# Dealing GpSimd's power and multiplication of the q and k norms out over three turns of an attention pipeline

## The reference

```python
q = (x @ Wq).reshape(b, n, H, DH).transpose(0, 2, 1, 3)
k = (x @ Wk).reshape(b, n, H, DH).transpose(0, 2, 1, 3)
...
q = l2norm(q)
k = l2norm(k)
dots = jnp.einsum('bhid,bhjd->bhij', q, k) * QK_SCALE
dots = jnp.einsum('hg,bgij->bhij', W_pre_th, dots)
...
top = jax.lax.top_k(dots, TOPK)[0]
vk = top[..., -1:]
dots = jnp.where(dots < vk, mask_value, dots)
attn = jax.nn.softmax(dots, axis=-1)
attn = jnp.einsum('hg,bgij->bhij', W_post_th, attn)
```

## Time and profile before

| | us |
|---|---|
| median of 3 runs | 2283.63 (2280.85 to 2287.51) |
| the profiled execution | 2286.81 |
| its span, first to last instruction | 2285.0 |
| attention's first and last power (L1381) start | 220.7 and 1937.9 |

### The profile page before, as it was taken

One profiled execution on the slowest core, in us unless ns is written; L12 is line 12 of the kernel. 1 busy time (PEld: TensorE's weight loads), 2 busy tenths in 40 slices (PEclk: granted clock), 3 DMA queues, 4 the chain that ended last, 5 costly groups with the idle time before them and its releaser, 6 DMA issues. The chain is left out here.

```text
span 2285.0 us, 55636 instructions
## 1 busy us (share of the span) xinstructions
PE 2040.8 (89%) x16059; PEld 1325.7 (58%) x16060; DVE 1765.2 (77%) x6818; ACT 1602.4 (70%) x4676; POOL 938.0 (41%) x2739
## 2 busy tenths in 40 slices
PE   7995799899989998899899988998899889974997
PEld 3433456666666666666666666666666666663433
DVE  6565389968996899689968996899689958984346
ACT  4442589858985888589768875897689768951542
POOL 3001455454544554555355435553554356321000
PEclk9997799999999999999999999999999999997998
DMA  6002012111211121112111211121112101302002
GB/s 180 0 0 88 18 46 63 44 26 44 63 44 26 44 63 44 26 44 63 44 27 44 63 44 26 45 62 44 26 45 63 44 24 48 70 24 89 1 0 74
DMA packets 113219, 104.72 MB, mean 46 GB/s; under 512 B 34448, under 2 KB 110864, under 8 KB 112912
## 3 DMA queue, kind: packets, MB, share of 16 engines
q1 hardware_dynamic: 108000, 96.65, 16.6%
q10 hardware_dynamic: 4912, 4.46, 0.6%
HBM read 19.14 MB, written 12.71 MB: 14 GB/s over the span
## 5 line engine op out<-in xcount | busy, mean ns | idle before, releaser
L1054 PE MATMUL bankC<-R,E 128*128 128x128 f32 x2560 | 352.0, 287 | 46.9 <-POOL R L1416 46.9
L1054 PEld LDWEIGHTS bankC<-R,E 128*128 128x128 f32 x2560 | 338.3, 202 | 85.1 <-POOL R L1416 51.8
L1038 PE MATMUL bankB<-raw,mixpre 128*128 128x76 f32 (+37 forms) x1024 | 354.7, 434 | 20.4 <-DMA raw<-SC 20.3
L1254 ACT ACTIVATE S<-bankB,aim_first 128x68 f32<-128x68 f32 (+56 forms) x456 | 232.8, 514 | 87.8 <-PE bankB L1038 87.2
L1514 DVE TENSOR_SCALAR_CACHE_REDUCE S<-S,minus_thr 128x68 f32<-128x68 f32 (+56 forms) x456 | 217.7, 514 | 94.1 <-POOL minus_thr L1400 93.5
L1391 POOL TENSOR_TENSOR S<-S,diagmask 128x8 f32<-128x8 f32 x512 | 116.6, 233 | 409.1 <-ACT S L1254 353.0
L1568 DVE SCALAR_TENSOR_TENSOR E<-S,limit,E 128x68 f32<-128x68 f32 (+56 forms) x456 | 234.1, 549 | 37.6 <-ACT E L1280 9.0
L1416 POOL TENSOR_SCALAR R<-mixpost,rinv 128x128 f32<-128x128 f32 x512 | 187.6, 379 | 183.8 <-DVE rinv L1572 183.4
L1027 PE MATMUL bankD<-KT,QT 64*64 64x132 f32 (+8 forms) x2304 | 190.5, 405 | 66.5 <-ACT SC L1243 37.4
L1280 ACT ACTIVATE E<-S,nmax 128x12 f32<-128x12 f32 (+56 forms) x512 | 241.7, 535 | 0.0
L1080 PEld LDWEIGHTS bankM<-PT,V 128*64 128x64 f32 x5120 | 180.3, 138 | 97.9 <-issue 90.5
(11 more groups left out here) (178 smaller groups left out, 3927.7 us busy)
## 6 DMA issues: line engine op xcount, KB each, us to landing
X_first<-in_L_attn_x_dram ACTq DMA_DIRECT2D x8, 512.0 KB, 9.7
x<-X_first SPq DMA_DIRECT2D x8, 512.0 KB, 2.9
xt<-x SPq DMA_DIRECT2D x32, 128.0 KB, 2.3
x<-xt SPq DMA_DIRECT2D x32, 128.0 KB, 2.4
X_last<-x SPq DMA_DIRECT2D x8, 512.0 KB, 6.6
out_dram<-X_last SPq DMA_DIRECT2D x8, 512.0 KB, 2.8
raw<-SC SPq DMA_DIRECT2D x8, 258.0 KB, 3.0
raw<-SC SPq DMA_DIRECT2D x8, 254.0 KB, 3.0
```

Source lines behind the costliest of these rows:

```text
L1038: last = nc.tensor.matmul(bankB[n % 2][:, 0:wide(n)], W.mixpre[:, :], raw[n % RAWS][:, 0:wide(n)], start=True, stop=True)
L1054: last = nc.tensor.matmul(bankC[n % 2][:, jb * P:(jb + 1) * P], E[n % EBUFS][:, jb * P:(jb + 1) * P], R[n % RBUFS][:, :], start=True, stop ...
L1254: nc.scalar.activation(S[n % SBUFS][:, 0:wide(n)], src, ACT.Identity, bias=W.aim_first[:, group(n)]).then_inc(S_out, 1)
```

## The change

`norm` is cut in two: `inverse_norms` (wait for the sums, power) and `norm` (wait for the power and for the evicted projection, multiplication). In a tile the power of q stays in turn 2; the multiplication of q and the power of k stand in turn 4; the multiplication of k stands in turn 6. The work ahead of the loop keeps its order.

```diff
-            def norm(j, i):
+            def inverse_norms(j, i):
                 pool.wait_ge(ssq_done, 2 * j + i + 1)
                 nc.gpsimd.tensor_tensor(rn[:, i, :], ssq[:, i, :], W.neghalf[:, 0:H], ALU.pow).then_inc(rn_ready, 1)
+
+            def norm(j, i):
                 pool.wait_ge(rn_ready, 2 * j + i + 1)
                 wait_read(pool, ("qk"[i], j, 1))
                 v = qk[:, i, :].rearrange("p (h d) -> p h d", d=DH)
...
-            norm(0, 0)
-            norm(0, 1)
+            for i in range(2):
+                inverse_norms(0, i)
+                norm(0, i)
...
                     if g == 2:
                         copy_halo(t + 1)
+                        inverse_norms(t + 1, 0)
+                    if g == 4:
                         norm(t + 1, 0)
-                    if g == 4:
+                        inverse_norms(t + 1, 1)
+                    if g == 6:
                         norm(t + 1, 1)
```

## The result

| | before | changed |
|---|---|---|
| median of 4 runs, us | 2282.93 (2280.85 to 2287.51) | 2301.07 (2299.65 to 2304.03) |
| the profiled execution, us | 2286.81 | 2299.65 |
| its span, us | 2285.0 | 2297.9 |

The changed kernel takes 1.0078 of the time, with a 95% interval of 1.006 to 1.0097: it is **slower by some 18 us**. The forecast was 2315 us, slower by 31; the direction and the range (2292 to 2328) held, the step was forecast 1.7 times too large.

The account below looks back on a forecast made before the run. VectorE was taken to set the pace from late tile 1 through tile 3, TensorE in tile 0. Terms 9.6 + 6.8 + 11.3 + 3.6 = 31.3 us slower gave a median of 2315 us, range 2292 to 2328.

Parts of the forecast that it names:

- The mechanism: VectorE sets the pace from late tile 1 through tile 3; multiplications right behind R stall its non-scan instructions until they end.
- Rival (c): L1527 and L1532 not held at all, stalls of tiles 1 and 2 vanish: faster, 2269 us; chance 0.08.
- Rival (b): Only TensorE pays: stalls cancel, late transposition costs 0.45 and 0.85 us in tiles 0 and 1: 2294 us; chance 0.09.
- Rival (a): Trade one for one: as many multiplications stall VectorE as before, TensorE's gaps absorb the late transposition: about 2284 us; chance 0.13.
- Tile 1: Second tile of each batch element: q's stall nets nothing, k's multiplication costs 1.2 us, eight times: 9.6 us.
- Tile 2: Third tile: L1556 stall gone (-1.58), q's multiplication 1.3, k's at L1527 1.1; +0.85 us, eight times: 6.8 us.
- Tile 3: Widest tile: k's multiplication stalls L1527 0.86 us, q's costs 0.75 at L1490; 1.6 us, seven times: 11.3 us.
- The race at L1490: Tile 3: q's multiplication and L1490 start 0.04 us apart; stall of 1.69 us or nothing, 0.75 taken.
- In tiles 2 and 3 VectorE does not wait for them: Turn 4's nmax, masks and thresholds come 1.9 us earlier, but VectorE is not waiting there; no gain booked.
- tile 3 lengthened most: Sign of a right forecast in the new profile: tile 3 grows most, by 0.9 or 2.5 us.
- Tile 0: First tile, where TensorE sets the pace: its transposition waits 0.45 us for k's multiplication, eight times: 3.6 us.
- The power: GpSimd's 2.9 us power, run in turns 2 and 4, holds no VectorE instruction; priced at nothing on VectorE.

Follow-up runs that it names:

- q late alone: Changed kernel with the multiplication of k put back to turn 4 behind its power, only that of q later than before: 2310.37 us, ratio 1.012 to the kernel before.
- isolated run: Kernel before with the change made in one tile of four only: tiles 1 alone 2286.93 us (ratio 1.001), tiles 2 alone 2293.11 us (ratio 1.0039).

## Why the prediction was right, and its size wrong

**The mechanism** held: VectorE sets the pace in tiles 1 to 3, and a multiplication that runs when VectorE comes to a flip holds it to its end. The instructions that the prediction named beforehand are the ones that are held: L1533 with 0.82 to 1.68 us in tiles 1 to 3, L1538 in tile 1; L1562 has no instance over 0.21 us, and L1574 of tile 1 is normal. Rival (c), that L1527 and L1532 aren't held, fell by the first row of tile 1. Rival (b) fell with q late alone; TensorE's waits are real, 0.18 and 0.62 us a tile and 8.5 us in sum over those of before (15.2 us in 18 places against 6.7 in two), near what (b) had for them, but most of it stands in tiles 1, where VectorE sets the pace. Rival (a), one for one, was half right: the first stalls of tiles 1 and 2 did only move, but each of the two tiles got a second one, and tile 3 one where it had none.

**Tile 1** was forecast at 8 x 1.2 = 9.6 us. The isolated run has 1.22 in the sixth batch element and 9.4 for all eight, the whole change 9.6 in its profiled execution. The mechanism is the forecast's too: the stall at L1538 is 1.6 us, the wait of 0.29 us for a threshold behind it is gone in both traces, and about 1.2 a tile is left.

**Tile 2** was forecast at -1.58 + 1.3 + 1.1 = 0.85. The isolated run has -1.58 + 2.37 = 0.79. In the whole change the tile is lengthened by less, 0.5 in the sixth batch element and 3.2 us for all eight instead of 6.8, since there the multiplication of q holds the flip for 0.7 to 1.1 us in seven tiles (and L1538 for 1.6 in the eighth); in the sixth batch element it is 1.08 where the isolated run has 1.35. The stall that the change removes was read in one batch element: it is at L1556 in five of the eight tiles, and at L1551 in the other three, for 1.0 to 1.7 us.

**Tile 3 is the step that failed**: 7 x 1.6 = 11.3 us forecast, and 1.6 us in sum by the marks of the profiled execution. Of the 1.6, two tiles that had the long form before and have the short one now gave back 1.2 us each; against the short form's length the seven are 4.8 us longer, 0.25 to 0.52 in six and 2.24 in one. The multiplication of k is not the error: it holds L1533 for 0.8 us in all seven, 0.86 forecast. Two other parts were wrong. The race at L1490, of which I took the middle, "since 0.04 us separate them", is no coin toss: VectorE starts first in six of seven tiles, because R ends 0.2 us after it (1554.65 + 0.72 against 1555.12), and pays nothing that it had not paid before; it loses once, 1.6 us. I had booked 0.75 us seven times, 5.3 us (and the middle of 1.69 and nothing is 0.85). I took the order from one tile, where the two were nearest. And "In tiles 2 and 3 VectorE does not wait for them" (the thresholds) was read from the second batch element as well. In the other batch elements it does; the kernel before, timeline of VectorE in tile 3 of the first:

```profile
429.40 0.69 DVE L1514 TENSOR_SCALAR_CACHE_REDUCE S<-S,minus_thr 128x460 f32<-128x460 f32 x1 [0.27 <-POOL minus_thr L1400]
```

It waits 0.27 us in three tiles 3, 0.56 in one and 1.6 in the two of the long form, and part of the 0.8 us stall at L1527 takes the place of this wait, as tile 1's does of its own. (One gap of 0.34 us, at 608.39 in tile 2, was missed by "no gap over 0.3 us".) Over the kernel VectorE waits 85.8 us for thresholds in 44 places, where it waited 93.5 in 59. Its stalls grew by some 24 us and these waits shrank by 7.7, of which some 3 are the two long waits of tiles 3; I take the rest as the part of the stalls that cost nothing; the tile with the wait at 1108.90 above shows it for one hold, no run for the sum. So "tile 3 lengthened most" was wrong: tile 1 is, with 9.6 us against 4.8.

**Tile 0** was forecast at 8 x 0.45 = 3.6 us; TensorE's wait is 0.18 behind the first tile, and 2.23 in the first. Its multiplication started at 725.93 and TensorE was ready at 727.71, 1.8 us later, where by the earlier trace rows I had 1.5. The seven waits of 0.18 sum to 1.3; the first tile's 2.23 does not show at its end, which is at 300.1 us in both traces. By the marks the eight tiles 0 are 0.7 us longer in sum, forms mixed.

In sum the intervals came to 9.6 + 3.2 + 1.6 + 0.7 = 15.1 us in the profiled execution instead of 31.3. The two profiled executions differ by 12.8, since the changed kernel is 1.3 us faster to its first mark and 0.9 behind its last. The medians differ by 18: the profiled execution of the kernel before lay 3.9 us above its median, the changed one's 1.4 below. Tiles 0 and 3 in the other form, at 2 and 1.6 us each, are of that size, but which form they had in the executions without a profile is not on record. So the marks show where the terms were too large, and the last few microseconds stay open. One slip of the working changes little: with 1.3 us as its end, tile 2's term is 10.4 us, not 9.6, and the range ends at 2328.3.

**The power** was priced at nothing, and 16 more of them measured at nothing. The Trainium skill ("SBUF — State Buffer", section "Who interferes with whom") has GpSimd hold the shared port pair for a whole instruction. The trace agrees for the multiplications, down to the end of the held instruction (539.79 against 539.77). It does not agree for the power of 128x16: 2.91 us of it beside L1530 and L1535 in the forms that are held elsewhere, with not 0.1 us lost. Here the measurement decides.

## What to carry to other kernels

An idle engine's work is not free where it holds the busy engine's instructions: count its instructions by what the busy engine starts while they run, and look for short instructions with a maximum ten times their median, which is how such holds appear in a profile. Spreading work evenly over turns says nothing; here it put the multiplications of tiles 1 to 3 beside the flips, which don't pass, where most had been beside the scans, which do, and in these tiles the long holds of a batch element went from two to five. Then look for a wait behind each hold: where one is as long, the hold is free, and taking it away wins nothing. And read a race, or the absence of a wait, from all the tiles that take part: both of my errors came from one batch element out of eight.

## What I had not expected of the hardware

- **The length of a GpSimd instruction does not tell whether it holds.** A multiplication of 1.26 us on 128x640 holds a flip of two elements for 0.53 us; a power of 2.91 us on 128x16 holds nothing. Whether the operation or the amount of data decides was not tested.
- **Pieces don't let VectorE in for free.** A multiplication of 128x256 takes 0.61 us and one of 128x1024 1.90; four pieces take 2.49 us in a row, the held instruction gets in only between two pieces, and the next piece can hold the next one: three in a row lost 0.9 us.
- **The same eight matmuls take 3.67 or 5.37 us**, at a granted clock of 1.00 or 0.69, behind the same wait, and how many of the seven tiles 0 go which way differs between kernels from one to six. The change in tile 1 alone costs 10 us by its stalls and measured as 3 through that, so an isolated part is read from its own tile before its median.
